# Identity products added at nine places of the tensor queue in a four-layer transformer kernel

## The reference

```python
x = x + _L0_attn_ref(_layernorm(x), ...)   # flow
x = x + _L0_ffn_ref(_layernorm(x), ...)    # gated
x = x + _L1_attn_ref(_layernorm(x), ...)   # narrow
x = x + _L1_ffn_ref(_layernorm(x), ...)    # mixture
```

## Time and profile before

| | us |
|---|---|
| median of 3 runs | 1187.87 |
| lowest and highest run | 1185.0, 1188.53 |
| the profiled execution's own time | 1188.62 |
| its span in the trace | 1187.0 |
| TensorE matmul busy in it | 1065.8 (90%) |
| VectorE busy | 900.5 (76%) |
| ScalarE busy | 715.9 (60%) |
| GpSimd busy | 401.4 (34%) |

### The profile page before, as it was taken

One profiled execution on the slowest core, in us unless ns is written; L12 is line 12 of the kernel. 1 busy time (PEld: TensorE's weight loads), 2 busy tenths in 40 slices (PEclk: granted clock), 3 DMA queues, 4 the chain that ended last, 5 costly groups with the idle time before them and its releaser, 6 DMA issues. The chain is left out here.

```text
span 1187.0 us, 18638 instructions
## 1 busy us (share of the span) xinstructions
PE 1065.8 (90%) x6893; PEld 552.2 (47%) x6893; DVE 900.5 (76%) x1583; ACT 715.9 (60%) x1218; POOL 401.4 (34%) x254
## 2 busy tenths in 40 slices
PE   5379859999999999999879999999999779999996
PEld 3256655455555455555412222222222257888885
DVE  7958577866666676767777899999999058787777
ACT  5323536433433454433357888888888779788784
POOL 1127502777686776778522200000010011221200
PEclk9559989999999999999969999999999979999998
DMA  4000010000000000100010110000010012313001
GB/s 96 1 1 3 1 36 1 1 10 1 1 1 2 1 2 1 55 27 2 1 44 15 53 43 20 23 14 28 15 20 1 1 37 61 102 55 105 36 36 36
DMA packets 30657, 29.35 MB, mean 25 GB/s; under 512 B 10784, under 2 KB 26280, under 8 KB 29544
## 3 DMA queue, kind: packets, MB, share of 16 engines
q1 hardware_dynamic: 30568, 28.17, 8.0%
HBM read 23.57 MB, written 4.26 MB: 23 GB/s over the span
## 5 line engine op out<-in xcount | busy, mean ns | idle before, releaser
L1997 ACT ACTIVATE narrow_att_probs<-psum 128x512 f32<-128x512 f32 x512 | 264.9, 603 | 61.3 <-PE psum L1922 61.1
L2017 DVE TENSOR_REDUCE front_maxima<-psum 128x1 f32<-128x1024 f32 x240 | 281.9, 1219 | 19.9 <-PE psum L1031 15.6
L1276 POOL TENSOR_TENSOR gated_tally<-gated_probs,gated_tally 128x1024 f32<-128x1024 f32 x96 | 231.0, 2406 | 77.5 <-ACT gated_probs L1535 69.0
L1535 ACT ACTIVATE gated_probs<-psum 128x1024 f32<-128x1024 f32 x128 | 124.1, 1022 | 159.5 <-PE psum L1423 156.9
L1637 DVE TENSOR_REDUCE gated_maxima<-psum 128x1 f32<-128x512 f32 x256 | 164.6, 685 | 50.2 <-PE psum L1313 49.0
L1922 PE MATMUL psum<-narrow_att_q,narrow_att_k 50*128 50x512 bf16 x448 | 146.0, 384 | 5.9 <-ACT narrow_att_probs L1997 5.4
L1031 PE MATMUL psum<-narrow_att_k,narrow_att_q 48*128 48x512 bf16 x448 | 132.6, 381 | 11.3 <-DVE front_maxima L2017 2.5
L1935 PE MATMUL psum<-narrow_att_probs,narrow_att_v_ones 128*32 128x512 f32 x1024 | 138.1, 612 | 0.1
L2463 DVE TENSOR_TENSOR moe_hidden_lo<-moe_hidden,moe_hidden_hi 128x512 fp32r<-128x512 f32 x144 | 102.0, 733 | 47.1 <-ACT moe_hidden_hi L2368 46.4
L1436 PE MATMUL psum<-gated_probs,gated_values 128*64 128x512 f32 x512 | 132.1, 610 | 0.0
L2364 ACT ACTIVATE moe_hidden<-psum,back_up_bias 128x512 f32<-128x512 f32 x144 | 96.2, 689 | 32.4 <-PE psum L73 31.6
(11 more groups left out here) (393 smaller groups left out, 1931.1 us busy)
## 6 DMA issues: line engine op xcount, KB each, us to landing
moe_mixb<-moe_mix_scratch SPq DMA_DIRECT2D x8, 1024.0 KB, 4.9
narrow_parts_scratch<-gated_values SPq DMA_DIRECT2D x12, 128.0 KB, 2.1
narrow_parts_scratch<-narrow_att_part SPq DMA_DIRECT2D x12, 128.0 KB, 2.2
narrow_att_q<-narrow_parts_scratch SPq DMA_DIRECT2D x14, 96.0 KB
narrow_att_q<-narrow_parts_scratch SPq DMA_DIRECT2D x42, 32.0 KB
narrow_att_k<-narrow_parts_scratch SPq DMA_DIRECT2D x14, 96.0 KB
narrow_att_k<-narrow_parts_scratch SPq DMA_DIRECT2D x42, 32.0 KB
X<-in_L_attn_inputs SPq DMA_DIRECT2D x4, 256.0 KB, 3.8
```

The costliest lines, as they stand in the source:

```text
L1276: pool.tensor_tensor(tally[:, n % 2, :, :], probs[:, kt % 4, :, :], so_far, ALU.add).then_inc(tallied, 1)
L1535: act.activation(probs[:, k % 4, :, :], psum[:, 2 * e:2 * e + 2, :], ACT.Exp, scale=SCALE).then_inc(exped, 1)
L1997: act.activation(probs[:, k % 3, 2 * e + u % 2, :], psum[:, SCORE_BANK + j % 3, :], ACT.Exp, scale=SCALE).then_inc(exped, 1)
L2017: dve.tensor_reduce(maxima[:, n % 2, at:at + 1], chunk.rearrange("p a b -> p (a b)"), AX.X, ALU.max).then_inc(chunk_used, 1)
```

## The change

A helper `fill` is added, which multiplies the float32 identity with its own first columns, writes to a place in PSUM that nobody reads, and signals nothing. It is called at these places of the tensor queue:

- mass stage, 64 columns each: 7 after `head_sums(1, 2)`; a new wait for VectorE's step `used1_1`, then 20, ahead of `head_sums(1, 3)`; per batch 6 and 12 behind the carry product, 8 behind the spread of r_sink, 4 and 10 behind the spread of comp. That is 75 in all.
- 128 columns each: 28 at the end of the second block of the flow layer; 16, 6 and 3 at the beginning of the gated layer, around its first two turns; 3 behind `nshift`, 6 behind the last `den` and 8 at the end of the gated layer; 2 behind each of the narrow layer's six lead pairs; 5, 5 and 7 ahead of the mixture's first three turns, and 5 ahead of `gate_logits`.

```diff
+def fill(pe, C, out, count):
+    for _ in range(count):
+        pe.matmul(out, C["ident"], C["ident"][:, 0:out.shape[1]], start=True, stop=True, skip_group_check=True)
...
                 spread(1, sink)
+                unused = [psum[:, 4 * b + 1, HALF_B + P + P // 2:] for b in range(BATCH)]
                 pe.wait_ge(step, AT["p1_2"])
                 head_sums(1, 2)
+                fill(pe, C, unused[0], 7)
+                pe.wait_ge(step, AT["used1_1"])
+                fill(pe, C, unused[0], 20)
                 pe.wait_ge(step, AT["p1_3"])
                 head_sums(1, 3)
                 for b in range(BATCH):
                     pe.wait_ge(step, AT[f"cum_give{b}"])
                     pe.matmul(psum[:, 4 * b, HALF_B + P:HALF_B + P + 1], carry_w[:, :], cum_give[:, b, P - 1:P],
                               start=True, stop=True, skip_group_check=True).then_inc(carry_done, 1)
+                    fill(pe, C, unused[b], (6, 12)[b])
                     pe.wait_ge(step, AT[f"carried{b}"])
                     spread(b, r_sink)
+                    fill(pe, C, unused[1 - b], 8)
                     pe.wait_ge(step, AT[f"comp{b}"])
                     pe.wait_ge(fac_copied, b + 1)
                     spread(b, comp)
+                    fill(pe, C, unused[1 - b], (4, 10)[b])
...
                 down(3)
+                fill(pe, C, psum[:, 4, 0:P], 28)
...
+            fill(pe, C, psum[:, SUM_BANK, 0:P], 16)
             turn_quarter(0)
+            fill(pe, C, psum[:, SUM_BANK, 0:P], 6)
             turn_quarter(1)
+            fill(pe, C, psum[:, SUM_BANK, 0:P], 3)
             for job in lead[:4]:
                 project(job)
...
-            small(tail)
+            for job in tail:
+                small([job])
+                fill(pe, C, psum[:, 0, 0:P], {("nshift",): 3, ("den", HALVES - 1): 6}.get(job, 0))
+            fill(pe, C, psum[:, 0, 0:P], 8)
...
                 for c in lead:
                     for x in range(2):
                         maximum(c, x)
+                    fill(pe, C, psum[:, SUM_BANK, 0:P], 2)
...
             for q in range(QUARTERS - 1):
+                fill(pe, C, psum[:, 3, 0:P], (5, 5, 7)[q])
                 turn_quarter(q)
...
                 if k == GATES_AT:
+                    fill(pe, C, psum[:, 5, 0:P], 5)
                     gate_logits()
```

## The result

The changed kernel takes **1210.97 us** (median of 6 runs, 1208.28 to 1212.04), the kernel before beside it 1188.2 us: ratio 1.0197, 95% interval 1.0179 to 1.0216. The forecast was 1203 with a range up to 1207; the time is 8 us over the one and 4 us over the other.

The account below looks back on a forecast made before the run. The mass stage's end was taken as bound by a chain across VectorE, ScalarE and the tensor queue. Terms 20.3 - 0.6 - 1.1 - 2.0 - 1.8 = +14.8 on 1187.87 gave 1203 us; own range 1197 to 1208, with rivals 1178 to 1207.

Parts of the forecast that it names:

- term 4: Narrow layer's beginning: fills keep the clock up, so mixes run warm; -2.0 us, bounds -3 and +1.
- term 1: Mass stage: fills at 0.427 us on a clock that stays low overrun their waits and delay the chain; +20.3 us.
- term 5: Mixture: the gate logits run warm, about 1.8 us instead of 3.6; -1.8 us, bounds +0.8 and -2.
- Term 2: Seam and gated layer's beginning: fills fit their waits, turns and first projections run at full clock; -0.6 us.
- Term 3: Gated layer's end: fills hold the clock through two waits, so turn and output records run warm; -1.1 us.
- the clock rises with the fills: Rival, mass stage: clock up from about 57 us, stage +3.0, second block -4.7; 1181 us, chance 0.20.
- Half price by width: Rival: columns, not weight loads, bound a mass-stage fill, 0.21 us cold; the clock rises; 1175 us, chance 0.12.
- The later gains fail: Rival: after the mass stage's +20.3 the clock falls between fillings anyway, 0 to +2 more; 1209 us, chance 0.06.

Follow-up runs that it names:

- lead_only: The kernel before with only the twelve fills of the narrow layer's lead added: 1191.51 us, ratio 1.0042.
- warm_rest: hold_warm plus the change's fills at the seam, the gated layer's beginning and end and the mixture, without lead fills: 1179.54 us, ratio 0.9938.
- warm_lead: warm_rest plus narrow-layer lead fills: none behind the first chunk, twelve behind the second, two behind each later one: 1178.44 us, ratio 0.9913.
- mass_fit: The kernel before with only 13 mass-stage fills of 64 columns, counts fitted to the waits at the low clock's price: 1187.16 us, ratio 0.9997.
- experiment 9: The kernel before, unchanged, run again for a second profile, with stages compared over all profiles: 1185.67 us.
- before_again: The second profile of the kernel before, nothing changed: 1185.67 us, span 1184.1.
- hold_warm: The kernel before with only mass-stage fills, 104 of 120 columns in thirteen waits, from the first long wait on: 1180.89 us, ratio 0.9951.
- no_mass_no_lead: The changed kernel without the mass stage's fills and without the narrow layer's twelve lead fills: 1186.33 us, ratio 0.9996.
- mass_wide: The changed kernel with its 75 mass-stage fills 120 columns wide instead of 64, counts and places kept: 1189.92 us, ratio 1.0024.
- seam_narrow: no_mass_no_lead with the fills at the seam and the gated layer's beginning 64 columns wide instead of 128, counts kept: one run, 1189.7 us.

## Why the prediction was right in direction and wrong in size

**The term that failed is term 4**, the narrow layer's beginning: -2.0 forecast, +3.8 in the profile, outside its bounds (-3 to +1). "Cold, the twelve lead fills only stand in VectorE's shadow or delay it by up to 1" left out the rate. VectorE takes a chunk every 1.17 us (9.40 / 8), of which two cold scores need 0.96 to 1.03, so some 0.15 us a round were free, and two cold fills want 0.87 by my own price. That makes a pause in every round, 0.7 us by these figures and 0.89 measured. lead_only shows them alone: five pauses that sum to 3.84 us, and +4.7 in the stretch against the first profile of before. The step before it failed as well: that the clock would hold. The clock was up at the layer's start and fell at 620 us. Two fills cover 0.5 us of a wait that is 2.74 us long in warm_rest, which has none there; in warm_lead twelve stand in it, and the clock stays up until all of the lead is done. And had it held, the gain would not have been 2 us but about none, as warm_lead shows: the mixes I counted at 0.88 us each stand behind the lead, where the clock falls again. The term is off by 5.8 of the 6.6 us between the forecast change of +14.8 and the spans' +21.4. The medians differ by 22.8.

**The upper end of the range failed too, and by its own sum.** The lower end is about what the terms' lower bounds add up to (1198.6 us); the upper one is not. +22 and +1 of term 1, 0 and 0, +1 of term 4 and +0.8 of term 5 make +24.8, or 1212.7 us and not 1208. The measured 1210.97 lies inside that sum and outside what was stated, although term 4 passed its own bound by 2.8 us.

**Term 1 (+20.3) was right in mechanism, short by 1.6.** A fill took 11.72 / 27 = 0.434 us, for 0.427. Against the kernel before, the starts moved by 6.5, 2.2, 2.3, 5.8, 2.3 and 2.9 us where I had 6.2, 2.0, 2.0, 5.4, 2.0 and 2.7: 0.2 of the first is a later start of the whole stage, the other chains are 0.2 to 0.4 us longer each, of which the fill's price explains 0.1 at most (16 x 0.007). What the remainder is was not taken apart. The clock stayed low throughout, as forecast from the load-bound and cold stretch of the earlier trace rows. mass_fit shows that nothing else is in it.

**Term 2** (-0.6, bounds 0 to -1.3): VectorE's first maxima of the gated layer came 12.43 us after the layer's start and not 13.70, at the bound; over the profiles with these fills at full width it is 12.4 to 13.4, over those without 13.7 to 14.4. **Term 3** (-1.1): -1.1 by the rows after, against this profile of before; but four profiles without the fills have these products warm as well (experiment 9), so that it too is a gain in some executions only. **Term 5** (-1.8): -1.7 against this profile; but before_again, lead_only and hold_warm have the same 27.7 us without fills, so it is a gain in some executions. no_mass_no_lead, with the fills of terms 2, 3 and 5 alone, gained nothing that the measurement can tell (0.9996).

**The rivals.** That the clock rises with the fills did not happen, yet its mechanism was real: mass_wide does just that, and its block is worth what the rival said (-4.6 for -4.7), its mass stage costs more (+6.2 for +3.0): 1.4 of that lies ahead of the first fill (the head sums of 52.27 us start at 53.65), and 4.8 comes from the fills, though the clock rose when the rival said (57.3 us). What the two kernels differ in was not in my list of what speaks for and against: the columns of the product. Half price by width fell, 0.434 us against 0.21: 120 columns cost the same as 64. On that price the Trainium skill, "TensorE: Matmul & The Clock Gate", section "LDWEIGHTS (loading the stationary operand)", gives a load as its columns divided by 1.2 GHz, from which 107 ns for 128 columns is an estimate; this case agrees at the upper level (0.113 us in the earlier trace rows, 0.119 in hold_warm) and not at the lower one (0.217 us a record). The prediction read from it that a fill would be bound by its columns, and no run bears that out. The Trainium skill's same page, section "The HAM clock gate", says that activity releases the throttle; here 40 us of a 99% busy queue of narrow products did not, and 2.6 us of wide ones did.

"The later gains fail", with 1209 us and a chance of 0.06, came nearest in number, and it is right in that the clock fell between the lead's fillings; what it had at 0 to +2 was then made up of a loss of 3.8 in the lead and of gains at the other places.

**What stays open.** Which property of the wide product the clock answers to was not taken apart further: only 64 against 120 or 128 columns were run. Nor is width all: the second block begins with products of 512 columns, and in the kernel before the clock stayed at 0.50 there for 12.20 us, the queue busy for 11.50 of them. Why the clock's rise in the second block falls into two groups (3, or 11 to 12 us behind its start) from execution to execution was not settled. How much of term 2 lies on the path at the median I can't tell; warm_rest less hold_warm is 1.35 us by medians with overlapping intervals.

## What to carry to other kernels

A filler product is real work for the queue behind it: size its count by its price at the clock it will run at, against the wait it stands in, and check that the next real product's row still shows an idle time ended by the engine it waits for. Make it wide: in these runs, at equal cost, the clock stayed low under products of 64 columns (and fell from its upper level), and came up under those of 120. And start where the clock is still high: cover the first long wait so that it never falls; a few fills that are too short for their wait give a cold filler ahead of a critical consumer, which is worse than none.

## What I had not expected of the hardware

- A plain float32 product of the identity (two records) with 64 columns costs 0.434 us at 1.2 GHz and 0.227 us at 2.4 GHz (6.36 / 28 in seam_narrow); with 128 columns 0.229 us at 2.4 GHz (6.42 / 28 in no_mass_no_lead, the same chain). Half the columns save next to nothing.
- Chains that keep the queue equally full did opposite things to the clock: with 64 columns 40 us at 0.50, with 120 up to 1.00 about 2.6 us behind the first.
- Where a cold stretch ends differs between executions of the same work: before and lead_only are the same up to the narrow layer, and the second block took 100.77 and 97.42 us. Whether a kernel that is nearly always warm is steadier is not shown: warm_lead (mean clock 0.99) went from 1177.62 to 1179.48 us, but that is five runs against 29.
